# A product and its raw copy moved within a batch: the linear branch of a fused attention kernel

## The chip, the cores and the metric

The kernel runs on one core of a Trainium2 chip. Its time is the device time of one execution in microseconds. Five engines of the core work side by side, each through its own list of instructions in order, and wait for each other with semaphores: TensorE (PE: matrix products, writes PSUM), VectorE (DVE), ScalarE (ACT), GpSimd (POOL) and SyncE (SP, which issues the DMAs).

## The reference

32 batches of x (256 rows of 128 channels). Each batch is normalised, goes through an attention with 16 heads of 8 channels, and through one of eight dense layers, and both are added to x. The attention has two branches over the same q, k and v. Cut to these:

```python
q = _layernorm(q, q_gamma, q_beta)
k = _layernorm(k, k_gamma, k_beta)
scores = jnp.einsum('bhnd,bhmd->bhnm', q, k) / jnp.sqrt(jnp.float32(D))
aw = jax.nn.softmax(scores, axis=-1)
kth = jax.lax.top_k(aw, topk)[0][..., -1:]          # topk = 12 of 256
aws = aw * (aw >= kth)
o_s = jnp.einsum('bhnm,bhmd->bhnd', aws / (aws.sum(-1, keepdims=True) + 1e-08), v)
qf = jax.nn.softmax(q, axis=-1)
kf = jax.nn.softmax(k, axis=-1)
kv = jnp.einsum('bhnd,bhne->bhde', kf, v)
z = jnp.einsum('bhnd,bhd->bhn', qf, kf.sum(axis=2))
o_l = jnp.einsum('bhnd,bhde->bhne', qf, kv) / (z[..., None] + 1e-06)
o = a * o_s + (1.0 - a) * o_l
return o @ Wproj.T + bproj
```

The sparse branch (o_s) keeps the 12 largest of 256 weights in each row. The linear branch (o_l) has no scores: its numerator and its z are one product of the query features qf with kv, the "linear product" below.

## The kernel before, in words

The kernel is written out engine by engine. For each engine a function `body(it, par, xr)` is called for it = -2 to 31, and in it a loop runs over eight slots, u_ = 0 to 7. The order of the work is the order of the statements in these functions; nothing else schedules it. In one slot, four tiles of scores (two heads, two halves of the rows, 128x256 each) pass each stage.

What the engines do in a slot, for the work that matters here:

- VectorE: MAX8 over the four score tiles (`top`, line 656), then for the tiles of the slot before: replace the eight largest (`rest`, 663, with a load of the eight values `e8`) and MAX8 over what is left (`next8`, 669). Slot 2 also masks kv (line 677), slot 3 also takes a maximum of qkn (682).
- GpSimd: `drop` = top minus its own first element (414), then `gap` and `below` (439, 443), a flag for each weight that is not kept. In slots 0 to 3 it also normalises q and k of the next batch (355, 361), the last step of which writes `qkn` in slot 3.
- ScalarE: a copy `kept` of the turned tiles (841), slot by slot different copies out of PSUM, four exponentials `e` with their row sums (881), the exponentials `e8` of the eight largest (886), then more copies, and its share of `below` (956).
- TensorE: `turn(u_)` transposes the weights of four slots ago and puts the dropped ones far below zero (1051, 1052), in every second slot `product(u_)` multiplies the kept weights with v (1073), then `early(u_)`, the scores for the next slot (1033), and `late(u_)`.

One PSUM bank, `work_ps`, serves in turn for a row of small products that the batch needs beside its scores: qf turned (slot 0), kv (slot 1), the linear product (line 1176), the transposes of qkn for the next batch (1186, slot 3), remainders of a split into bf16 parts, v, the next x turned, and the next q and k (1155, slot 7). Each writer waits for the one before it to have been copied out. For the linear product the semaphores are: `kv_ready` (VectorE has masked kv), `w_lin` (TensorE is done), `lin_copied` (ScalarE has copied the bank into `lin_raw`, a part of the tensor `over`, line 859). The transposes of qkn wait for `lin_copied` and for `qkn_ready` of GpSimd. ScalarE copies them into `part` (865), and SyncE's DMAs write the parts to memory and load them back as the queries and keys of the next batch.

Of the kernel before, what the change touches and what calls it, by code (L numbers as in the profile page):

```python
# [30 lines left out]
P = 128  # L31
H = 16
# [3 lines left out]
NT = N // P  # L36
# [11 lines left out]
VA = D + 1  # L48
# [22 lines left out]
def wait(engine, semaphore, value):  # L71

    if isinstance(value, int) and value <= 0:
        return None
    return engine.wait_ge(semaphore, value)
# [9 lines left out]
def build(nc, x, Wqkv, bqkv, q_gamma, q_beta, k_gamma, k_beta, alpha, Wproj, bproj, W, bW, logits, u, y):  # L85
# [12 lines left out]
    def exists(batch):  # L98
        return not isinstance(batch, int) or 0 <= batch < B

    with ExitStack() as ctx:
# [68 lines left out]
        kv = sb("kv", [P, H, VA])  # L170
        qfT = sb("qfT", [P, N])
# [3 lines left out]
        sums_sb, lin_raw = over[:, 0:NT * H], over[:, NT * H:2 * NT * H]  # L175
# [11 lines left out]
        e = sb("e", [P, RING, TILES, N])  # L187
# [14 lines left out]
        work_ps = ps("work_ps", [P, 512])  # L202
# [578 lines left out]
        def _(act):  # L781
# [48 lines left out]
            def body(it, par, xr):  # L830
                nxt = 1 - par
                for u_ in range(UNITS):
# [20 lines left out]
                        nc.scalar.copy(osT[:], pv_ps[:, 0:N]).then_inc(s["osT_copied"], 1)  # L853
                    if u_ == 1 and (exists(it + 1) or exists(it + 2)):
                        rsqrt_steps(it)
                    if u_ == 3 and exists(it):
                        act.wait_ge(s["w_lin"], it + 1)
                        wait(act, s["lin_ready"], it)
                        nc.scalar.copy(lin_raw.rearrange("p g e -> p (g e)"), work_ps[:, 0:NT * H * VA]).then_inc(
                            s["lin_copied"], 1)  # L860
                    if u_ == 4 and exists(it + 1):

                        act.wait_ge(s["w_qkT"], it + 2)
# [9 lines left out]
                    if exists(it):  # L873
# [11 lines left out]

                        nc.scalar.activation(e8[:, u_ % 2], drop[:, u_ % 2, :, 1:9], ACT.Exp).then_inc(s["e8_ready"], 1)  # L886

                    if u_ in (0, 4) and exists(it - 1):
                        act.wait_ge(s["pv_ready"], it * QUADS + (u_ - 6) // 2 + 1)

                        if u_ == 0:
                            wait(act, s["w_turn"], it - 2)
                        nc.scalar.copy(oT[:, nxt, u_ // 4].rearrange("p a n -> p (a n)"), pv_ps[:]).then_inc(
                            s["pv_copied"], 1)
# [112 lines left out]
        def _(pe):  # L1007
# [8 lines left out]
            def body(it, par, xr):  # L1016
# [61 lines left out]
                def sums():  # L1078

                    pe.wait_ge(s["pv_copied"], QUADS // 2 * it)  # L1080
                    for t in range(NT):
                        for q in range(QUADS):
                            at = (t * QUADS + q) * 4 * VA
                            mm(pv_ps[:, at:at + P], oT[:, nxt, q // 2, 1 - q % 2, t * P:(t + 1) * P], gather[:],
                               start=(t == 0 and q == 0), stop=False, is_transpose=True, skip_group_check=True)
                    if it == 1:
                        pe.wait_ge(s["eps_ready"], 1)
                    mm(pv_ps[:, 0:NT * H * VA].rearrange("p (g e) -> p g e", e=VA)[:, :, D], eps_ident[:],
                       z[:, nxt].rearrange("p t h -> p (t h)"), start=False, stop=True,
                       skip_group_check=True).then_inc(s["w_turn"], 1)  # L1090


                def remainder(p):
# [2 lines left out]
                    mm(work_ps[:], minus_one[:], part[:, p].rearrange("p a n -> p (a n)"), start=False,  # L1096
                       stop=True, skip_group_check=True).then_inc(s["w_rest"], 1)

                def early(u_):
                    if u_ == 0 and exists(it):  # L1100

                        pe.wait_ge(s["dexp_ready"], it + 1)
                        if exists(it + 1):
                            pe.wait_ge(s["raw_ready"], it + 2)
                        else:
                            pe.wait_ge(s["v_copied"], it + 1)
                        for t in range(NT):
                            last = nc.tensor.transpose(work_ps[:, t * P:(t + 1) * P], qk_exp[:, par, t, 0, :], ident[:])
                        last.then_inc(s["w_qfT"], 1)
                    if u_ == 1 and exists(it - 2):  # L1110

                        pe.wait_ge(s["osp_ready"], it - 1)
                        pe.wait_ge(s["lin_ready"], it - 1)
                        pe.wait_ge(s["pv_copied"], QUADS // 2 * it - 1 if exists(it - 1) else QUADS // 2 * B)
                        for t in range(NT):
                            dst = pv_ps[:, t * P:(t + 1) * P]
                            mm(dst, o_sparse[:, t, :], ident[:], start=True, stop=False, is_transpose=True)
                            last = mm(dst, lin[:, par, t, :], ident[:], start=False, stop=True, is_transpose=True)
                        last.then_inc(s["w_osT"], 1)
                    if u_ == 3 and exists(it - 2):  # L1120

                        pe.wait_ge(s["osT_copied"], it - 1)
                        pe.wait_ge(s["bout_ready"], 1)
                        pe.wait_ge(res_loaded[par], 16 * ((it - 2) // 2 + 1))
                        for t in range(NT):
                            dst = pv_ps[:, t * C:(t + 1) * C]
                            mm(dst, ident[:], x_res[:, par, t, :], start=True, stop=False)
                            mm(dst, xnT[:, (xr - 2) % XRING, t * P:(t + 1) * P], w_sel[:], start=False, stop=False)
                            mm(dst, ones3[:], bias3[:, 3 * C:4 * C], start=False, stop=False)
                            last = mm(dst, osT[:, t * P:(t + 1) * P], w_proj[:], start=False, stop=True)  # L1130
                        last.then_inc(s["w_out"], 1)
                    if u_ == 5 and exists(it + 1):

                        remainder(1)
                    if u_ == 6 and exists(it + 1):

                        if it == -1:
                            pe.wait_ge(s["wv_ready"], 1)
                            pe.wait_ge(s["bv_ready"], 1)
                        pe.wait_ge(s["part_ready"], PARTS * (it + 2))  # L1140
                        for t in range(NT):
                            dst = work_ps[:, t * C:(t + 1) * C]
                            mm(dst, xnT[:, (xr + 1) % XRING, t * P:(t + 1) * P], w_v[:], start=True, stop=False)  # L1143
                            last = mm(dst, ones3[:], bias3[:, 2 * C:3 * C], start=False, stop=True)
                        last.then_inc(s["w_v_ready"], 1)
                    if u_ == 7 and exists(it + 2):

                        pe.wait_ge(s["xT_copied"], it + 4)
                        if it == -2:
                            pe.wait_ge(s["wqk_ready"], 1)  # L1150
                            pe.wait_ge(s["pool_const"], 7)
                            pe.wait_ge(s["gather_ready"], 4)
                        for t in range(NT):
                            dst = work_ps[:, t * 2 * C:(t + 1) * 2 * C]
                            mm(dst, xnT[:, (xr + 2) % XRING, t * P:(t + 1) * P], w_qk[:], start=True, stop=False)  # L1155
                            if it == -2 and t == 0:
                                pe.wait_ge(s["bqk_ready"], 1)
                            last = mm(dst, ones3[:], bias3[:, 0:2 * C], start=False, stop=True)
                        last.then_inc(s["w_qk_ready"], 1)

                def late(u_):
                    if u_ == 1 and exists(it):
# [6 lines left out]
                        last = mm(work_ps[:, 0:H * VA], ones_row[:], eps_row[:].rearrange("o h e -> o (h e)"),  # L1169
                                  start=False, stop=True)  # L1170
                        last.then_inc(s["w_kv"], 1)
                    if u_ == 2 and exists(it):

                        pe.wait_ge(s["kv_ready"], it + 1)
                        for t in range(NT):
                            last = mm(work_ps[:, t * H * VA:(t + 1) * H * VA], qfT[:, t * P:(t + 1) * P],  # L1176
                                      kv[:].rearrange("p h e -> p (h e)"), start=True, stop=True)
                        last.then_inc(s["w_lin"], 1)
                    if u_ == 3 and exists(it + 1):

                        wait(pe, s["lin_copied"], it + 1)
# [39 lines left out]
                for u_ in range(UNITS):  # L1221
                    if exists(it if u_ >= 4 else it - 1):
                        turn(u_)
                    if u_ % 2 == 0 and exists(it if u_ >= 6 else it - 1):
                        product(u_)
                    if u_ == 5 and exists(it - 1):
                        sums()
                    early(u_)
                    if exists(it if u_ < UNITS - 1 else it + 1):
                        scores(u_)  # L1230
                    late(u_)
                    if (it, u_) == (-2, 7):
                        other_weights()
# [126 lines left out]
```

## Time and profile before

| | before |
|---|---|
| time, median of three runs | 1180.96 us (1179.04 to 1184.93) |
| time of the profiled execution | 1181.1 us |
| its span, first to last instruction | 1179.3 us |
| VectorE busy | 1148.9 us (97%) |
| ScalarE busy | 1063.5 us (90%) |
| GpSimd busy | 995.5 us (84%) |
| TensorE busy | 942.5 us (80%) |
| linear product on TensorE, idle before it | 40.4 us in 32 batches, released by VectorE's kv |
| transposes of qkn on TensorE, idle before them | 34.6 us, mostly released by GpSimd's qkn |
| copy of the linear product on ScalarE | 13.2 us in 32 batches, 411 ns each |
| mean granted TensorE clock | 0.992 of full speed |

All times below are from one profiled execution, in microseconds from the start of its span. "Busy" is the time in which an engine's instructions run; they overlap a little from one to the next, so starts are the safer numbers. The word behind an arrow in square brackets is what ended the idle time ahead of an instruction, as the profile infers it. A batch takes some 35 us of the span, a slot some 4.4.

### The profile page before, as it was taken

How to read it: one execution, taken by the hardware profiler on the slowest of the kernel's cores; microseconds unless marked ns; L12 is line 12 of the kernel's file. 1: busy time of each engine (PE TensorE's matmuls, PEld its weight loads, DVE VectorE, ACT ScalarE, POOL GpSimd, SP SyncE). 2: the span in 40 equal slices, each digit the busy share in tenths (PEclk: the TensorE clock that was granted, in tenths of full speed). 3: DMA queues.
4: the chain of work that ended last, by engine and by line, in shares of the span. 5: the costliest groups of instructions: out<-in, count | busy, mean ns of one | idle time of the engine just before them, and what ended most of it. 6: DMA issues, size and time to landing. Idle time of an engine off the chain costs nothing.

```text
span 1179.3 us, 34136 instructions
## 1 busy us (share of the span) xinstructions
PE 942.5 (80%) x9061; PEld 653.6 (55%) x9092; DVE 1148.9 (97%) x4358; ACT 1063.5 (90%) x3474; POOL 995.5 (84%) x1973
## 2 busy tenths in 40 slices
PE   4578878888888888888888888888887888888887
PEld 1355556555555555555555555555555555555555
DVE  7999999999999999999999999999999999999997
ACT  3689989999999999999999999999999989999986
POOL 6688888888889888889888888888888888889865
PEclk9999999999999999999999999999999999999999
DMA  3112321223321222231223231223221223321220
GB/s 100 46 55 82 86 86 38 77 61 86 87 84 39 70 68 86 86 87 37 77 60 86 86 86 45 70 59 86 86 86 48 67 61 86 86 82 38 71 63 13
DMA packets 165122, 82.74 MB, mean 70 GB/s; under 512 B 7737, under 2 KB 164927, under 8 KB 164930
## 3 DMA queue, kind: packets, MB, share of 16 engines
q1 hardware_dynamic: 164658, 80.43, 23.8%
q8 instruction: 74, 1.21, 0.4%
q14 instruction: 118, 0.97, 0.3%
q10 hardware_dynamic: 272, 0.13, 0.0%
HBM read 42.78 MB, written 37.75 MB: 68 GB/s over the span
## 4 chain that ended last, share of the span: by engine, by line
POOL 30%; ACT 24%; issue 18%; PE 17%; DVE 10%; DVEq 1%; POOLq 0%; DMA 0%; ACTq 0%; SPq 0%
ACT e L881 14%; POOL gap L439 10%; POOL below L443 5%; DVE top L656 4%; PE work_ps L1155 3%; DVE rest L663 3%; POOL qkn L361 3%; PE turn_ps L1051 3%; PE pv_ps L1073 3%; POOL qk_b L361 3%; POOL drop L414 2%; PE work_ps L1143 2%; POOL sq_half L424 2%; ACT part L910 2%; PE work_ps L1186 2%
## 5 line engine op out<-in xcount | busy, mean ns | idle before, releaser
L881 ACT ACTIVATE e<-score_ps,drop 128x256 f32<-128x256 f32 x1024 | 474.6, 492 | 32.3 <-POOL drop L414 32.2
L1051 PE MATMUL turn_ps<-ident,e 128*128 128x128 f32 x2016 | 382.9, 284 | 40.1 <-ACT kept L841 20.5
L663 DVE MATCH_REPLACE8 rest<-e 128x256 f32<-128x256 f32 x1020 | 411.6, 407 | 0.0
L669 DVE MAX8 next<-rest 128x8 f32<-128x256 f32 x1020 | 405.7, 413 | 0.5 <-issue 0.3
L656 DVE MAX8 top<-score_ps 128x8 f32<-128x256 f32 x1024 | 360.0, 413 | 10.2 <-PE score_ps L1033 10.0
L439 POOL TENSOR_SCALAR gap<-e,next 128x256 bf16<-128x256 f32 x794 | 368.9, 479 | 0.1
L1052 PE MATMUL turn_ps<-minus_huge,below 128*128 128x128 bf16 x2016 | 363.1, 221 | 0.0
L1051 PEld LDWEIGHTS turn_ps<-ident,e 128*128 128x128 f32 x2016 | 286.6, 142 | 72.4 <-issue 44.1
L841 ACT ACTIVATE kept<-turn_ps 128x1024 f32<-128x1024 f32 x252 | 266.9, 1059 | 36.6 <-PE turn_ps L1052 36.6
L443 POOL TENSOR_SCALAR below<-gap 128x768 bf16<-128x768 bf16 (+1 forms) x254 | 216.7, 853 | 41.7 <-POOL gap L439 41.7
L881 ACT ACTIVATION_READ_ACCUMULATOR e<-score_ps,drop 128x1 f32 x1024 | 230.6, 225 | 0.0
L1052 PEld LDWEIGHTS turn_ps<-minus_huge,below 128*128 128x128 bf16 x2016 | 215.1, 107 | 0.7
L1073 PE MATMUL pv_ps<-kept,v_aug 128*32 128x256 f32 x2000 | 134.9, 387 | 20.4 <-ACT over L900 20.2
L414 POOL TENSOR_TENSOR drop<-top 128x36 f32<-128x36 f32 x256 | 62.8, 245 | 91.9 <-DVE top L656 88.5
L956 ACT ACTIVATE below<-e,next 128x256 bf16<-128x256 f32 x222 | 123.7, 557 | 0.0
L1033 PE MATMUL score_ps<-k_slots,q_slots 64*128 64x256 bf16 x1024 | 103.0, 278 | 16.3 <-issue 10.1
L1073 PEld LDWEIGHTS pv_ps<-kept,v_aug 128*32 128x32 f32 x2000 | 55.0, 110 | 62.4 <-issue 42.8
L663 DVE MATCH_VALUE_LOAD rest<-e 128x8 f32 x1020 | 74.9, 73 | 3.4 <-ACT e L886 3.1
L1033 PEld LDWEIGHTS score_ps<-k_slots,q_slots 64*128 64x128 bf16 x1024 | 30.8, 94 | 72.4 <-issue 65.0
L886 ACT ACTIVATE e<-drop 128x32 f32<-128x32 f32 x256 | 66.6, 260 | 0.0
L1155 PE MATMUL work_ps<-w_qk,xnT 128*128 128x256 f32 x128 | 46.8, 449 | 20.4 <-ACT xnT L942 20.4
L1176 PE MATMUL work_ps<-kv,qfT 128*128 128x144 f32 x128 | 24.8, 317 | 40.4 <-DVE kv L677 40.4
(229 smaller groups left out, 1398.3 us busy)
## 6 DMA issues: line engine op xcount, KB each, us to landing
part_slots<-part SPq DMA_DIRECT2D x128, 192.0 KB, 2.3
q_slots<-part_slots SPq DMA_DIRECT2D x64, 256.0 KB, 3.4
k_slots<-part_slots SPq DMA_DIRECT2D x64, 256.0 KB, 3.9
part_slots<-part SPq DMA_DIRECT2D x64, 128.0 KB, 1.9
x_sb<-in_L_attn_x SPq DMA_DIRECT2D x32, 128.0 KB, 3.9
x_res<-in_L_attn_x SPq DMA_DIRECT2D x32, 128.0 KB, 4.0
out_y<-out_sb SPq DMA_DIRECT2D x32, 128.0 KB, 4.1
w_ops<-in_L_ffn_W SPq DMA_DIRECT2D x1, 512.0 KB
```

The lines of the kernel that those rows point to most:

```text
L439: nc.gpsimd.tensor_scalar(gap[:, half, t, :], e[:, r, t, :], -1.0, next8[:, r, t, TOPK - 9:TOPK - 8], ALU.mult, ALU.add).then_inc(s["gap_s ...
L443: nc.gpsimd.tensor_scalar(below[:, r, 0:many], gap[:, half, 0:many], HUGE, 0.0, ALU.min, ALU.max).then_inc(s["below_pool"], many)
L656: nc.vector.max(top[:, q, t, 1:9], score_ps[:, q, t // 2, t % 2, :]).then_inc(s["top_ready"], 1)
L663: nc.vector.match_replace(rest[:, t, :], e8[:, (u_ - 1) % 2, t, :], e[:, (u_ - 1) % RING, t, :], REMOVED).then_inc(s["rest_ready"], 1)
L669: nc.vector.max(next8[:, (u_ - 1) % RING, t, :], rest[:, t, :]).then_inc(s["next_ready"], 1)
L841: nc.scalar.activation(kept[:, u_ % 4], turn_ps[:], ACT.Relu).then_inc(s["turn_copied"], 1)
L881: nc.scalar.activation(e[:, u_ % RING, t, :], score_ps[:, u_ % 2, t // 2, t % 2, :], ACT.Exp, bias=drop[:, u_ % 2, t, 0:1], accum_out=z[:, ...
L956: nc.scalar.activation(below[:, r, t, :], e[:, r, t, :], ACT.Relu, scale=-1.0, bias=next8[:, r, t, TOPK - 9:TOPK - 8]).then_inc(s["below_a ...
L1033: last = mm(score_ps[:, v_ % 2, hh, nt, :], q_slots[rows, side, v_, nt * P:(nt + 1) * P], k_slots[rows, side, v_, :], start=True, stop=True)
L1051: mm(dst, e[:, r, t, keys], ident[:], start=True, stop=False, is_transpose=True)
L1052: last = mm(dst, below[:, r, t, keys], minus_huge[:], start=False, stop=True)
L1073: last = mm(pv_ps[32 * j:32 * (j + 1), half * N:(half + 1) * N], v_aug[:, side, mc, 4 * q + j, :], kept[:, v_ % 4, j % 2, mc, :], start=(m ...
```

## The change

The linear product leaves the end of TensorE's slot 2, where it stood in `late`, and becomes a function `linear` that is called in slot 3 behind `turn(3)` and ahead of `early(3)`, the output product of the batch two before. Its copy on ScalarE stays in slot 3 but moves from ahead of the four exponentials of that slot to behind them and behind `e8`.

```diff
@@ ScalarE, body
-                    if u_ == 3 and exists(it):
-                        act.wait_ge(s["w_lin"], it + 1)
-                        wait(act, s["lin_ready"], it)
-                        nc.scalar.copy(lin_raw.rearrange("p g e -> p (g e)"), work_ps[:, 0:NT * H * VA]).then_inc(
-                            s["lin_copied"], 1)
                     if u_ == 4 and exists(it + 1):
...
                         nc.scalar.activation(e8[:, u_ % 2], drop[:, u_ % 2, :, 1:9], ACT.Exp).then_inc(s["e8_ready"], 1)
 
+                    if u_ == 3 and exists(it):
+                        act.wait_ge(s["w_lin"], it + 1)
+                        wait(act, s["lin_ready"], it)
+                        nc.scalar.copy(lin_raw.rearrange("p g e -> p (g e)"), work_ps[:, 0:NT * H * VA]).then_inc(
+                            s["lin_copied"], 1)
@@ TensorE, body
+                def linear():
+
+                    pe.wait_ge(s["kv_ready"], it + 1)
+                    for t in range(NT):
+                        last = mm(work_ps[:, t * H * VA:(t + 1) * H * VA], qfT[:, t * P:(t + 1) * P],
+                                  kv[:].rearrange("p h e -> p (h e)"), start=True, stop=True)
+                    last.then_inc(s["w_lin"], 1)
...
-                    if u_ == 2 and exists(it):
-
-                        pe.wait_ge(s["kv_ready"], it + 1)
-                        for t in range(NT):
-                            last = mm(work_ps[:, t * H * VA:(t + 1) * H * VA], qfT[:, t * P:(t + 1) * P],
-                                      kv[:].rearrange("p h e -> p (h e)"), start=True, stop=True)
-                        last.then_inc(s["w_lin"], 1)
...
                     if u_ == 5 and exists(it - 1):
                         sums()
+                    if u_ == 3 and exists(it):
+                        linear()
                     early(u_)
```

On TensorE, from the scores that end slot 2 to the turn of slot 4, before (the names are output<-inputs; `kv,qfT` is the linear product, `x_res,ident` begins the output product, `ident,qkn` are the transposes of qkn; in square brackets the semaphores waited for):

```order
L1176 MATMUL work_ps<-kv,qfT 128x144 [waits kv_ready]
L1051 MATMUL turn_ps<-ident,e 128x128 [waits turn_copied,below_act,below_pool]
...
L1127 MATMUL pv_ps<-x_res,ident 128x128 [waits even_res_loaded,bout_ready,osT_copied]
...
L1033 MATMUL score_ps<-k_slots,q_slots 128x256 [waits exp_done,slots_loaded]
L1186 MATMUL work_ps<-ident,qkn 128x128 [waits qkn_ready,lin_copied]
L1051 MATMUL turn_ps<-ident,e 128x128 [waits turn_copied,below_act,below_pool]
```

The same stretch after:

```order
L1051 MATMUL turn_ps<-ident,e 128x128 [waits turn_copied,below_act,below_pool]
...
L1103 MATMUL work_ps<-kv,qfT 128x144 [waits kv_ready]
L1135 MATMUL pv_ps<-x_res,ident 128x128 [waits even_res_loaded,bout_ready,osT_copied]
...
L1033 MATMUL score_ps<-k_slots,q_slots 128x256 [waits exp_done,slots_loaded]
L1187 MATMUL work_ps<-ident,qkn 128x128 [waits qkn_ready,lin_copied]
L1051 MATMUL turn_ps<-ident,e 128x128 [waits turn_copied,below_act,below_pool]
```

The linear product has changed places with the turn of slot 3; the rest stands as before.

On ScalarE, slot 3 and the start of slot 4, before (`over<-work_ps` is the copy of the linear product):

```order
L841 ACTIVATE kept<-turn_ps 128x1024 [waits turn_ready,pv_ready]
L859 COPY over<-work_ps 128x288 [waits lin_ready,w_lin]
L881 ACTIVATE e,z<-score_ps,drop 128x256 [waits turn_ready,drop_ready]
...
L886 ACTIVATE e<-drop 128x32
L920 COPY out_sb<-pv_ps 128x256 [waits w_out]
```

After:

```order
L841 ACTIVATE kept<-turn_ps 128x1024 [waits turn_ready,pv_ready]
L876 ACTIVATE e,z<-score_ps,drop 128x256 [waits turn_ready,drop_ready]
...
L881 ACTIVATE e<-drop 128x32
L886 COPY over<-work_ps 128x288 [waits lin_ready,w_lin]
L920 COPY out_sb<-pv_ps 128x256 [waits w_out]
```

The copy has moved behind five instructions; before and after it, ScalarE's order is unchanged.

## Rows read from the trace of the kernel before

**Rows 1.** Busy time by stretch: length, PE, PEld, DVE, ACT, POOL, clock, DMA, GB/s

```profile
110.00:1125.00 1015.00, 830.15 (x8114) 579.32 (x8143) 1005.91 (x3836) 946.66 (x3092) 885.16 (x1747) 0.99 0.25 71
```

**Rows 2.** Waits of VectorE over the span: us in total, times, longest

```profile
DVE top L656 <- PE score_ps L1033: 10.0, 14, 2.7
DVE rest L663 <- ACT e L886: 3.1, 9, 0.6
```

**Rows 3.** Chain of waits, 614 to 634 us: start, us, what

```profile
614.56 1.23 POOL qkn L361
...
631.36 0.40 ACT xnT L942
631.80 0.70 PE work_ps L1155 x2
...
633.55 0.35 PE score_ps L1033 x4
```

**Rows 4.** Timeline of TensorE, slots 2 to 4 of one batch

```profile
610.63 0.76 PE L1176 MATMUL work_ps<-kv,qfT 128*128 128x144 f32 x4 [1.45 <-DVE kv L677]
611.22 0.27 PE L1051 MATMUL turn_ps<-ident,e 128*128 128x128 f32 x1
...
614.78 0.40 PE L1033 MATMUL score_ps<-k_slots,q_slots 64*128 64x256 bf16 x4
615.93 0.63 PE L1186 MATMUL work_ps<-ident,qkn 128*128 128x128 f32 x4 [0.76 <-POOL qkn L361]
...
617.86 1.07 PE L1073 MATMUL pv_ps<-kept,v_aug 128*32 128x256 f32 x16
```

**Rows 5.** Timeline of ScalarE in the same batch

```profile
608.92 1.03 ACT L841 ACTIVATE kept<-turn_ps 128x1024 f32<-128x1024 f32 x1
...
614.00 0.41 ACT L859 COPY over<-work_ps 128x288 f32<-128x288 f32 x1
614.59 0.47 ACT L881 ACTIVATE e<-score_ps,drop 128x256 f32<-128x256 f32 x1 [0.18 <-POOL drop L414]
...
616.52 0.38 ACT L920 COPY out_sb<-pv_ps 128x256 f32<-128x256 f32 x1
...
621.23 0.24 ACT L886 ACTIVATE e<-drop 128x32 f32<-128x32 f32 x1
...
630.98 0.25 ACT L886 ACTIVATE e<-drop 128x32 f32<-128x32 f32 x1
```

**Rows 6.** Timeline of VectorE: the batch's first row, two loads, the next batch

```profile
599.22 1.10 DVE L656 MAX8 top<-score_ps 128x8 f32<-128x256 f32 x3 [0.26 <-PE score_ps L1033]
...
622.92 0.07 DVE L663 MATCH_VALUE_LOAD rest<-e 128x8 f32 x1
...
631.40 0.09 DVE L663 MATCH_VALUE_LOAD rest<-e 128x8 f32 x1
...
634.30 1.08 DVE L656 MAX8 top<-score_ps 128x8 f32<-128x256 f32 x3
```

**Rows 7.** Timeline of TensorE: batch 1, and a wait near the end

```profile
77.69 0.76 PE L1176 MATMUL work_ps<-kv,qfT 128*128 128x144 f32 x4 [1.59 <-DVE kv L677]
...
82.99 1.08 PE L1186 MATMUL work_ps<-ident,qkn 128*128 128x128 f32 x4 [2.68 <-POOL qkn L361]
...
86.23 1.07 PE L1073 MATMUL pv_ps<-kept,v_aug 128*32 128x256 f32 x16
...
1129.64 0.40 PE L1033 MATMUL score_ps<-k_slots,q_slots 64*128 64x256 bf16 x4 [3.22 <-ACT e L881]
```

**Rows 8.** Busy time by stretch as in rows 1; the clock stands ahead of DMA

```profile
80.00:85.00 5.00, 2.32 (x15) 1.86 (x15) 5.00 (x19) 3.93 (x13) 4.68 (x8) 0.74 0.02 5
1130.00:1132.50 2.50, 2.50 (x18) 1.82 (x16) 2.37 (x10) 0.61 (x4) 1.32 (x4) 0.55 0.52 153
```

**Rows 9.** Timeline of VectorE: first rows of batch 1 and batch 2

```profile
66.31 1.08 DVE L656 MAX8 top<-score_ps 128x8 f32<-128x256 f32 x3
...
102.67 1.41 DVE L656 MAX8 top<-score_ps 128x8 f32<-128x256 f32 x4
```

## Prediction

> **What bounds the kernel now.** I read the busy time of the long middle first. From 110 to 1125 us VectorE is busy for 1005.91 of 1015 us [rows 1]: the selection (four MAX8, four replacements, four MAX8 in each of eight slots of a batch) runs nearly without a break. So whatever is gained elsewhere can bring at most the 9.1 us that are left there. The reader might stop at "VectorE is the bound" and conclude that TensorE and ScalarE have room. The second view speaks against that. VectorE's few waits are all on the other engines: 10.0 us on scores, 3.1 us on the exponentials of the eight largest [rows 2].
>
> How near is the other side? The chain of waits answers it for one batch [rows 3]: GpSimd's last step of the normalisation (qkn, ends 614.56 + 1.23 = 615.79), TensorE's transposes of qkn 0.14 us later at 615.93 [rows 4], then ScalarE's copies and exponentials and TensorE's products of slots 4 to 7 in turn, down to ScalarE's xnT copy (631.36 to 631.76), the query and key product that it releases at 631.80 and the next batch's first scores at 633.55. In the last slot of that batch VectorE loads the eight values at 631.40, and the ScalarE instruction that makes them runs from 630.98 to 631.23 [rows 5, 6]: 0.17 us before, about what a handover takes (0.14 us at the transposes, 0.04 us from the xnT copy to its product). So from qkn to the end of the batch there is **a second loop of about the same length as VectorE's own**. The batch from 599.22 to 634.30 [rows 6] lasts 35.08 us, with both near their limit. A delay inside that second loop is paid by VectorE.
>
> **Part 1: the product moves behind the turn of slot 3 (TensorE).** Before, the linear product waits 1.45 us for kv at 610.63 and the turn follows at 611.22 [rows 4]. The wait has VectorE's kv step as releaser, a step that the change doesn't touch. After, the turn goes first. Its last input is the kept copy of slot 2, ScalarE 608.92 to 609.95 [rows 5]; with 0.14 us for the handover it starts at 610.09. kv is there before the turn is through, so the product (0.59 us, 610.63 to 611.22) follows at once; the turn and the output product take 611.22 to 614.78 = 3.56 us together, as now. The three end at 610.09 + 3.56 + 0.59 = 614.24, and the scores behind them (0.40 us) at 614.64. No instruction is added, no DMA moves, and TensorE has gained 0.54 us there. The gain comes to nothing, since what TensorE does next waits for something later (below), and the kept copy of slot 3, which the earlier turn releases, is followed on ScalarE by exponentials that wait for GpSimd anyway.
>
> **Part 2: the raw copy moves behind the exponentials of slot 3 (ScalarE).** Now it runs at 614.00 for 0.41 us, and the first exponential follows at 614.59 after 0.18 us of waiting for GpSimd's subtraction [rows 5]. That start is GpSimd's, so taking the copy away from the front does not bring the exponentials forward: the gain is 0. After, the copy takes the place that the output copy has now, right behind the eight values: 616.52 [rows 5], to 616.93. The output copy and one `below` slide by some 0.3 us into time in which ScalarE would wait for the turn of slot 4.
>
> **What waits for it.** The transposes of qkn write the PSUM bank that the copy reads, so TensorE waits there for `lin_copied` and for qkn. Before, the copy was over at 614.41 and qkn came last, at 615.79. After, the copy is last: 616.93 plus a handover of 0.04 to 0.14 us gives 616.97 to 617.07, against 615.93. I take 617.03, **1.10 us later in each batch** (bounds 1.04 and 1.14). Behind this wait stand, in TensorE's order, the turn of slot 4, the product and the scores of that slot; ScalarE's part copy, the exponentials of slot 4 and all that follows hang on the turn and the transposes. What is spare on the way is at the slot ends of VectorE, and in the last slot nothing is spare (above), so I count all of it. The change concerns the 31 batches that have a next one: 31 x 1.10 = 34.1 us.
>
> **What the longer wait does to TensorE's clock.** TensorE now waits 0.76 us before the transposes [rows 4]; after, from 614.64 to 617.03, 2.39 us, every batch. The trace has two waits above 2 us with the clock at its full level (2.4 GHz) before them: 2.68 us before 82.99 and 3.22 us before 1129.64 [rows 7]. In both places the granted clock then stands at the lower level of 1.2 GHz for some microseconds: 0.74 on the mean over 80 to 85 and 0.55 over 1130 to 1132.5 [rows 8]. The wait of 1.59 us before 77.69 was not followed by it: the linear product behind it has its usual 0.76 us [rows 4, 7]. 2.39 is nearer to 2.68, so I expect the fall in most batches.
>
> The price is in the same rows, since the wait at 82.99 is at this very place, in batch 1: from the start of the transposes to the product behind the turn it took 82.99 to 86.23 = 3.24 us, against 615.93 to 617.86 = 1.93 us at the full clock [rows 4, 7]: 1.31 us more. That batch is also a trial of the claim that a delay there is paid in full: from its first MAX8 to the next batch's it lasted 66.31 to 102.67 = 36.36 us [rows 9], 1.28 us above the 35.08 of the batch above. Where the clock falls only after the transposes have begun, part of the 1.31 is saved; at no fall all of it. I take three quarters, 1.0 us per batch: 31 x 1.0 = 31 us; bounds 0 and 31 x 1.31 = 40.6 us.
>
> The Trainium skill (TensorE: Matmul & The Clock Gate, section "What's actually happening") says that the ramp penalty is below 1% of a typical kernel's span, which would be under 11.8 us here. Batch 1 shows 1.31 us for one fall, and nothing in this trace shows many of them; by the page's rule the sum would be rival 1.
>
> **The sum.** The profiled execution took 1181.1 us (span 1179.3), beside a median of 1180.96. 1181.1 + 34.1 + 31 = 1246 us.
>
> **The rivals.**
> 1. *Late, but the clock holds or rarely falls.* For it: a wait of 1.59 us did not lower it, and 2.39 lies between; ahead of the wait stands the output product. Then 1181.1 + 34.1 = 1215, and with a fall in each fourth batch 1225 us. The page above is on this side.
> 2. *Faster.* The 1.45 us wait for kv and the copy ahead of the exponentials could have been what holds the batch, the copy then costing nothing behind. It decides itself at 615.79: if the exponentials of slot 3 and the copy are over by the time qkn is, the transposes are not late. They would have to end 1.1 us sooner, and their start is GpSimd's. At best VectorE's 9.1 us: 1172 us.
> 3. *VectorE has spare time enough.* The eight values of slot 4 are ready at 621.23 + 0.24 = 621.47 and are loaded at 622.92 [rows 5, 6], 1.45 us later, more than 1.10. If a later slot takes up the rest, the time stays within 1176 to 1187 us. Against it: the 0.17 us in the last slot, and batch 1. A half-way case (half of the delay taken up, no fall of the clock) gives 1198 us.
>
> **How the numbers follow.** The forecast, late with the clock falling in most batches (1226 to 1260): 0.62. Rival 1 (1208 to 1226): 0.23. The half-way case (1187 to 1208): 0.05. No change: 0.05. Faster: 0.03. Above 1260: 0.02. The range from 1210 to 1260 us holds some 0.84 of this: its low end is 31 x 1.04 = 32.2 us with a little taken up by VectorE's spare time, its high end 31 x (1.14 + 1.31) = 76 us, 1257, and a few us for other places. Faster or slower means by over 0.5%, about what a measurement of this kernel can tell from no change (1175 and 1187 us): faster 0.03, same 0.05, slower 0.92.
>
> **What the profile after would show.** TensorE's wait for kv is gone from the table of waits, and the turn of slot 3 starts right behind the kept copy of slot 2. The wait before the transposes of qkn is about 2.4 us and its releaser is ScalarE's copy, no longer GpSimd; the copy starts about 0.1 us behind the start of the eight values. VectorE's work stays as it is and its share of the span falls; its new waits are on ScalarE's eight values in the last three or four slots of a batch, about 2 us a batch. The row of the granted clock has values below 9, and its mean goes from 0.99 to about 0.95 (batch 1 lost 0.26 x 5 us in the stretch shown). Wrong would be: a copy that ends before qkn (step "what waits for it"), a wait of 2.4 us at an unchanged clock mean (the clock term), or batches still of 35.1 us though the transposes come 1.1 us late (the claim that all of it is paid).

## The result, and the profile after

The changed kernel takes 1244.91 us (median of four runs, 1241.1 to 1245.98) against 1181.8 us before: the ratio is 1.0522, with an interval of 1.05 to 1.0543. The change costs 63 us, some 2 us in each of the 31 batches that have a next one. The forecast was 1246.

The first view of the changed kernel is busy time by stretch, over the long middle and then over 8 us of one batch (that which begins at 479.35). The columns are those of [rows 1]; the clock is the third number from the end.

```profile
110.00:1185.00 1075.00, 868.10 (x8125) 601.33 (x8154) 1019.20 (x3846) 950.89 (x3097) 888.23 (x1751) 0.96 0.23 67
494.00:496.00 2.00, 1.03 (x9) 0.51 (x7) 2.00 (x11) 1.55 (x7) 2.00 (x4) 1.00 0.00 0
496.00:498.00 2.00, 0.90 (x7) 0.85 (x8) 2.00 (x6) 1.73 (x8) 1.84 (x4) 0.92 0.00 0
498.00:500.00 2.00, 2.00 (x15) 1.55 (x12) 2.00 (x10) 0.00 (x0) 1.80 (x5) 0.50 0.00 0
500.00:502.00 2.00, 2.00 (x22) 0.72 (x22) 1.79 (x8) 1.64 (x3) 1.83 (x5) 0.73 0.00 0
```

VectorE, nearly without a gap before (9.1 us of 1015, [rows 1]), now stands idle for 56 of 1075 us. The mean clock of the middle fell from 0.99 to 0.96, and the four short rows show how: TensorE works for half of 494 to 498, and from just before 498 to past 500 it is granted 0.50, the lower of its two levels.

The timeline of TensorE for the same batch answers to [rows 4]. In square brackets stand the idle time ahead and what ended it.

```profile
490.56 0.30 PE L1051 MATMUL turn_ps<-ident,e 128*128 128x128 f32 x1 [0.93 <-ACT kept L841]
...
491.96 0.71 PE L1103 MATMUL work_ps<-kv,qfT 128*128 128x144 f32 x4
...
494.64 0.40 PE L1033 MATMUL score_ps<-k_slots,q_slots 64*128 64x256 bf16 x4
497.10 0.66 PE L1187 MATMUL work_ps<-ident,qkn 128*128 128x128 f32 x4 [2.06 <-ACT over L886]
...
500.20 1.48 PE L1073 MATMUL pv_ps<-kept,v_aug 128*32 128x256 f32 x16
```

The linear product no longer waits. The transposes do, 2.06 us instead of 0.76, and what ends their wait is ScalarE's copy, no longer GpSimd's qkn. The turn behind them runs at the lower level: the product follows 3.10 us after the transposes' start, not 1.93.

ScalarE in the same stretch, to hold beside [rows 5]:

```profile
489.38 1.03 ACT L841 ACTIVATE kept<-turn_ps 128x1024 f32<-128x1024 f32 x1
...
494.69 0.48 ACT L876 ACTIVATE e<-score_ps,drop 128x256 f32<-128x256 f32 x1 [0.45 <-POOL drop L414]
...
496.51 0.25 ACT L881 ACTIVATE e<-drop 128x32 f32<-128x32 f32 x1
496.63 0.42 ACT L886 COPY over<-work_ps 128x288 f32<-128x288 f32 x1
...
500.36 1.02 ACT L841 ACTIVATE kept<-turn_ps 128x1024 f32<-128x1024 f32 x1 [2.64 <-PE turn_ps L1052]
```

The exponentials still start when GpSimd lets them: ScalarE waits 0.45 us for it, where it copied before. The copy ends at 497.05, the transposes start 0.05 us later, and ScalarE then stands idle for 2.64 us until the turn of slot 4 is there.

VectorE's waits through the rest of this batch:

```profile
502.20 1.43 DVE L656 MAX8 top<-score_ps 128x8 f32<-128x256 f32 x4 [0.41 <-PE score_ps L1033]
503.99 0.09 DVE L663 MATCH_VALUE_LOAD rest<-e 128x8 f32 x1 [0.37 <-ACT e L881]
508.75 0.09 DVE L663 MATCH_VALUE_LOAD rest<-e 128x8 f32 x1 [0.45 <-ACT e L881]
513.77 0.09 DVE L663 MATCH_VALUE_LOAD rest<-e 128x8 f32 x1 [0.60 <-ACT e L881]
516.98 1.42 DVE L656 MAX8 top<-score_ps 128x8 f32<-128x256 f32 x4 [0.23 <-PE score_ps L1033]
```

They add up to 2.06 us in one batch, spread over its second half: each time VectorE has caught up with the loop that starts at the transposes. Over the whole span the table of waits says the same, beside [rows 2]:

```profile
PE work_ps L1187 <- ACT over L886: 66.9, 31, 4.1
...
DVE rest L663 <- ACT e L881: 44.5, 86, 1.2
...
DVE top L656 <- PE score_ps L1033: 16.6, 34, 2.7
```

VectorE's two waits grew from 13.1 to 61.1 us. Two things could be behind that 63 us, late transposes and a slower TensorE, and the profile of one kernel shows them together. The experiments take them apart.

### The profile page after: what moved, and what is told of

The parts are those of the page before. It is cut to its first block, busy times and chain, and to the rows that moved or that the text cites. A ratio compares the mean times of both kernels' runs of the same rounds, so it can differ in the third digit from the quotient of the medians.

```text
span 1239.4 us, 34136 instructions
## 1 busy us (share of the span) xinstructions
PE 979.8 (79%) x9061; PEld 675.0 (54%) x9092; DVE 1160.0 (94%) x4358; ACT 1066.0 (86%) x3474; POOL 995.6 (80%) x1973
## 4 chain that ended last, share of the span: by engine, by line
ACT 31%; POOL 22%; PE 20%; issue 17%; DVE 8%; DMA 1%; DVEq 1%; POOLq 0%; ACTq 0%; SPq 0%
ACT e L876 19%; POOL gap L439 8%; PE turn_ps L1051 5%; POOL below L443 4%; DVE top L656 3%; PE work_ps L1163 3%; PE pv_ps L1073 3%; ACT kept L841 2%; DVE rest L663 2%; POOL qk_b L361 2%; PE turn_ps L1052 2%; PE work_ps L1187 2%; PE work_ps L1151 2%; POOL drop L414 2%; ACT below L956 2%
## 5 line engine op out<-in xcount | busy, mean ns | idle before, releaser
L1051 PE MATMUL turn_ps<-ident,e 128*128 128x128 f32 x2016 | 410.6, 297 | 64.4 <-ACT kept L841 47.2
L1052 PE MATMUL turn_ps<-minus_huge,below 128*128 128x128 bf16 x2016 | 387.9, 229 | 0.0
L1051 PEld LDWEIGHTS turn_ps<-ident,e 128*128 128x128 f32 x2016 | 302.3, 150 | 116.5 <-issue 61.2
L876 ACT ACTIVATION_READ_ACCUMULATOR e<-score_ps,drop 128x1 f32 x1024 | 241.2, 236 | 0.0
L1052 PEld LDWEIGHTS turn_ps<-minus_huge,below 128*128 128x128 bf16 x2016 | 224.6, 111 | 1.1 <-issue 0.2
L1073 PE MATMUL pv_ps<-kept,v_aug 128*32 128x256 f32 x2000 | 141.8, 403 | 21.6 <-ACT over L900 20.4
L956 ACT ACTIVATE below<-e,next 128x256 bf16<-128x256 f32 x222 | 127.4, 574 | 0.0
L1187 PE MATMUL work_ps<-ident,qkn 128*128 128x128 f32 x128 | 27.1, 348 | 72.8 <-ACT over L886 66.9
L881 ACT ACTIVATE e<-drop 128x32 f32<-128x32 f32 x256 | 69.8, 272 | 0.0
```

Of the source, the lines that this page charges most:

```text
L876: nc.scalar.activation(e[:, u_ % RING, t, :], score_ps[:, u_ % 2, t // 2, t % 2, :], ACT.Exp, bias=drop[:, u_ % 2, t, 0:1], accum_out=z[:, ...
L956: nc.scalar.activation(below[:, r, t, :], e[:, r, t, :], ACT.Relu, scale=-1.0, bias=next8[:, r, t, TOPK - 9:TOPK - 8]).then_inc(s["below_a ...
L1051: mm(dst, e[:, r, t, keys], ident[:], start=True, stop=False, is_transpose=True)
L1052: last = mm(dst, below[:, r, t, keys], minus_huge[:], start=False, stop=True)
L1073: last = mm(pv_ps[32 * j:32 * (j + 1), half * N:(half + 1) * N], v_aug[:, side, mc, 4 * q + j, :], kept[:, v_ % 4, j % 2, mc, :], start=(m ...
```

## The experiments

The theory: the copy behind the exponentials makes the transposes about 1.05 us late, which VectorE pays in full; and the wait that this leaves on TensorE lowers its clock in most batches, at some 1 us each. Rival A: all of the loss is the lateness, and the low clock costs nothing. Rival B: the product's new place on TensorE does the harm.

### The two moves apart

**e1_product_only** has the product in its new place and the copy in its old one:

```diff
+                    if u_ == 3 and exists(it):
+                        act.wait_ge(s["w_lin"], it + 1)
+                        wait(act, s["lin_ready"], it)
+                        nc.scalar.copy(lin_raw.rearrange("p g e -> p (g e)"), work_ps[:, 0:NT * H * VA]).then_inc(
+                            s["lin_copied"], 1)
                     if u_ == 4 and exists(it + 1):
...
                         nc.scalar.activation(e8[:, u_ % 2], drop[:, u_ % 2, :, 1:9], ACT.Exp).then_inc(s["e8_ready"], 1)
 
-                    if u_ == 3 and exists(it):
-                        act.wait_ge(s["w_lin"], it + 1)
-                        wait(act, s["lin_ready"], it)
-                        nc.scalar.copy(lin_raw.rearrange("p g e -> p (g e)"), work_ps[:, 0:NT * H * VA]).then_inc(
-                            s["lin_copied"], 1)
```

> Product in slot 3 behind the turn as in the changed kernel, its copy back ahead of the exponentials. Theory (late copy, then the clock): the product is over at 612.04 on the time axis of the prediction, ScalarE is free for the copy at 614.0 as before, the transposes of qkn wait for GpSimd again; 1181 us, +-5, clock mean 0.99. Rival (the product's new place holds TensorE up): 1215 us or more.

Measured: 1184.74 us, ratio to before 1.0004 (0.9992 to 1.0017). The move on TensorE costs nothing and brings nothing that this measurement can tell. Rival B is out. In its table of waits the transposes wait for GpSimd as before:

```profile
PE work_ps L1187 <- POOL qkn L361: 41.2, 31, 3.1
```

**e2_copy_only** is the other half: the product stays in `late(2)`, only the copy moves.

```diff
-                    if u_ == 3 and exists(it):
-                        act.wait_ge(s["w_lin"], it + 1)
-                        wait(act, s["lin_ready"], it)
-                        nc.scalar.copy(lin_raw.rearrange("p g e -> p (g e)"), work_ps[:, 0:NT * H * VA]).then_inc(
-                            s["lin_copied"], 1)
                     if u_ == 4 and exists(it + 1):
...
                         nc.scalar.activation(e8[:, u_ % 2], drop[:, u_ % 2, :, 1:9], ACT.Exp).then_inc(s["e8_ready"], 1)
 
+                    if u_ == 3 and exists(it):
+                        act.wait_ge(s["w_lin"], it + 1)
+                        wait(act, s["lin_ready"], it)
+                        nc.scalar.copy(lin_raw.rearrange("p g e -> p (g e)"), work_ps[:, 0:NT * H * VA]).then_inc(
+                            s["lin_copied"], 1)
```

> Product in slot 2 as before, its copy behind the exponentials as in the changed kernel. Theory: transposes 1.05 us late in each batch, 33 us in all; TensorE's wait ahead of them only 1.85 us, since the product still waits for kv in slot 2, so the clock falls in fewer batches: 1215 to 1240 us, clock mean 0.96 to 0.985. Rival (all of the loss is the lateness and what hangs on it, the clock costs nothing): as the changed kernel, 1245 us. Rival (the product's place): 1181 us.

Measured: 1246.42 us, ratio 1.0516 (1.0498 to 1.0535). The whole loss belongs to the copy. My expectation was a few us too low: I had counted on fewer falls of the clock with a wait of 1.8 us. One batch on TensorE:

```profile
495.28 0.40 PE L1033 MATMUL score_ps<-k_slots,q_slots 64*128 64x256 bf16 x4
497.49 1.11 PE L1186 MATMUL work_ps<-ident,qkn 128*128 128x128 f32 x4 [1.82 <-ACT over L886]
...
500.92 1.07 PE L1073 MATMUL pv_ps<-kept,v_aug 128*32 128x256 f32 x16
```

After 1.82 us of waiting the four transposes take 1.11 us, much as at 82.99 (1.08 us, [rows 7]), and the product comes 3.43 us after their start. By its time alone this run would fit rival A as well.

### Lateness without the slow clock

**e3_filled_wait** is the changed kernel, in which TensorE has something to do while it waits: it makes the scores of slot 3 five times over, the same values in the same place.

```diff
-                    for t in range(TILES):
+                    for t in list(range(TILES)) * (5 if u_ == 3 and it >= 0 else 1):
                         hh, nt = t // 2, t % 2
```

> The changed kernel, with the four score products of slot 3 issued five times over (the same values in the same place), so that TensorE works through most of its wait ahead of the transposes; no instruction that the others wait for is later than 616.3, VectorE needs these scores at 617.4. Theory: the transposes are still 1.05 us late, but the wait is some 0.8 us and the clock stays: 1215 us, +-6, clock mean 0.985 or more. Rival (the clock costs nothing): 1245 us. If the clock falls all the same: 1245 us with a mean near 0.96, and the test says nothing.

Measured: 1218.36 us, ratio 1.0275 (1.0251 to 1.03). One batch on TensorE:

```profile
489.24 1.27 PE L1033 MATMUL score_ps<-k_slots,q_slots 64*128 64x256 bf16 x20
491.74 0.66 PE L1187 MATMUL work_ps<-ident,qkn 128*128 128x128 f32 x4 [1.23 <-ACT over L886]
...
493.70 1.07 PE L1073 MATMUL pv_ps<-kept,v_aug 128*32 128x256 f32 x16
```

The busy time of its middle, with the clock ahead of the DMA share:

```profile
110.00:1160.00 1050.00, 859.45 (x8581) 603.91 (x8612) 1014.68 (x3844) 950.25 (x3101) 889.88 (x1751) 0.99 0.24 69
```

The transposes are as late as in the changed kernel, but the wait ahead of them is 1.23 us (0.8 had been expected), the clock keeps its mean of 0.99, and the product follows after 1.96 us. With more instructions on TensorE it loses 34.2 us on before, where the changed kernel loses 63.1. Rival A is out: it wanted 1245 us. So is any loss in proportion to lateness alone, since the lateness is the same and the loss is half.

### The slow clock without lateness

**e4_idle_no_delay** is the kernel before with a shorter output product, so that TensorE idles ahead of transposes that come no later than before. It leaves x, the dense layer and the bias out of the output of batches 0 to 29.

```diff
-                            mm(dst, ident[:], x_res[:, par, t, :], start=True, stop=False)
-                            mm(dst, xnT[:, (xr - 2) % XRING, t * P:(t + 1) * P], w_sel[:], start=False, stop=False)
-                            mm(dst, ones3[:], bias3[:, 3 * C:4 * C], start=False, stop=False)
-                            last = mm(dst, osT[:, t * P:(t + 1) * P], w_proj[:], start=False, stop=True)
+                            last = mm(dst, osT[:, t * P:(t + 1) * P], w_proj[:], start=True, stop=True)
```

> The kernel before, with the output product of slot 3 cut to its two products with w_proj: x itself, the dense layer and the bias are left out of the output of batches 0 to 29. Product and copy stand as before, so the transposes are not late, but TensorE is idle some 2.4 us ahead of them. Theory: the clock falls in most batches and costs about 1 us in each: 1205 to 1222 us, clock mean 0.95 to 0.97. Rival (the clock costs nothing): 1181 us.

Measured: 1200.05 us, ratio 1.0144 (1.009 to 1.0197): with less work some 16 us slower than before. The mechanism is there, 5 us short of the range that I gave. TensorE in a batch in which the clock fell and in one in which it didn't:

```profile
372.12 0.63 PE L1183 MATMUL work_ps<-ident,qkn 128*128 128x128 f32 x4 [2.37 <-POOL qkn L361]
...
375.12 1.56 PE L1073 MATMUL pv_ps<-kept,v_aug 128*32 128x256 f32 x16
...
408.44 0.63 PE L1183 MATMUL work_ps<-ident,qkn 128*128 128x128 f32 x4 [2.38 <-POOL qkn L361]
410.36 1.07 PE L1073 MATMUL pv_ps<-kept,v_aug 128*32 128x256 f32 x16
```

The busy time by stretch around the first of the two:

```profile
370.00:372.50 2.50, 0.38 (x4) 0.41 (x5) 2.50 (x12) 2.32 (x9) 2.50 (x5) 1.00 0.00 0
372.50:375.00 2.50, 2.50 (x19) 1.93 (x17) 2.50 (x9) 1.01 (x5) 2.34 (x4) 0.55 0.00 0
```

The same wait, the same releaser, and yet 3.00 us against 1.92 from the transposes to the product. So the length of the wait does not decide alone whether the clock falls; that the product comes about 1 us later where it falls shows directly. What this does to the batch is better read from many than from these two: the first lasts 36.30 us (from one first MAX8 to the next) and the second 35.17, but the same two batches last 35.91 and 35.18 in the kernel before, where the clock falls in neither. Over all batches of this run, those with a late product are 0.88 us longer than the others (table below).

### How much lateness, how much wait

Two more kernels put the copy between the exponentials of slot 3, the product where the change has it: behind the second (t == 1, below) and behind the third (t == 2).

```diff
                                                 ).then_inc(s["exp_done"], 1)
+                            if u_ == 3 and t == 1:
+                                act.wait_ge(s["w_lin"], it + 1)
+                                wait(act, s["lin_ready"], it)
+                                nc.scalar.copy(lin_raw.rearrange("p g e -> p (g e)"), work_ps[:, 0:NT * H * VA]).then_inc(
+                                    s["lin_copied"], 1)
...
```

> The changed kernel with the copy between the second and the third of the four exponentials of slot 3. Theory: the copy starts at 615.51, ends at 615.92, and the transposes start at 616.0, 0.1 us late; TensorE waits 1.4 us ahead of them, less than the 1.59 us that passed without a fall: 1184 to 1190 us, clock mean 0.985 or more. Rival (loss in proportion to lateness, 60 us for 1.05 us): 1187 to 1190 us. Rival (what costs is the copy being anywhere behind the first exponential): 1245 us.

Measured for **e5_after_two**: 1186.92 us, ratio 1.0027 (1.001 to 1.0043). The last rival, 1245 us, is out; the loss in proportion to lateness is not told from the theory here.

> The changed kernel with the copy between the third and the fourth exponential of slot 3. Theory: copy from 615.96 to 616.37, transposes at 616.45, 0.5 us late, 16 us in all; TensorE waits 1.8 us, as long as with the copy alone moved, where the clock fell in most batches: another 15 to 31 us, 1212 to 1232 us, clock mean 0.955 to 0.975. Rival (loss in proportion to lateness): 1214 us. Rival (lateness alone, no clock): 1200 us with a mean of 0.985 or more.

Measured for **e6_after_three**: 1218.87 us, ratio 1.0293 (1.025 to 1.0336). Lateness alone is out (1200 us; the clock mean of the profiled execution is 0.970 and not 0.985). The 1214 us of the loss in proportion lie inside the interval, 1212.7 to 1222.8, so it is e3 and not this run that speaks against it. In both the copy is what ends the wait of the transposes. From the table of waits of e5:

```profile
PE work_ps L1187 <- ACT over L883: 37.4, 31, 3.1
```

And from that of e6, 12 us more in the 31 batches:

```profile
PE work_ps L1187 <- ACT over L883: 49.0, 31, 3.6
```

All eight kernels side by side, from the timelines of their profiled executions, batches 1 to 30; the times stand beside 1184.15 us of before for e1 to e4 and 1183.09 for e5 and e6. The time is the median of all executions; the other columns come from the profiled one, which lies above the median in e5 (1190.4 us) and below it in e6 (1210.5) and after (1241.1). The start of the transposes, counted from the batch's first MAX8, and the wait are medians over the batches; "slow" are the batches in which the product comes over 2.2 us after the transposes' start (1.92 to 1.96 at the full clock); the last two columns are mean lengths of a batch, from one first MAX8 to the next.

| kernel | time, us | transposes start | wait ahead of them | slow batches | length, slow | length, others |
|---|---|---|---|---|---|---|
| before | 1181.8 | +16.69 | 0.75 | 1 of 30 | 36.36 | 35.43 |
| e1, product only | 1184.7 | +16.72 | 1.19 | 2 | 36.52 | 35.41 |
| e5, after two | 1186.9 | +16.72 | 1.08 | 4 | 36.86 | 35.55 |
| e4, idle, no delay | 1200.1 | +16.71 | 2.37 | 19 | 36.43 | 35.55 |
| e3, filled wait | 1218.4 | +17.77 | 1.23 | 1 | 37.56 | 36.59 |
| e6, after three | 1218.9 | +17.17 | 1.52 | 12 | 36.95 | 36.08 |
| after | 1244.9 | +17.75 | 2.06 | 21 | 37.69 | 36.84 |
| e2, copy only | 1246.4 | +17.77 | 1.83 | 21 | 38.01 | 36.75 |

Read down the last column: among the batches that are not slow, 0.48 us of lateness (e6) makes a batch 0.65 us longer, 1.08 us (e3) makes it 1.16 us longer. These batches can still hold a fall of the clock in another place. In e3, 20 of the 30 hold none at all and last 36.42 us on the mean, against 35.31 in the 24 such batches of before: 1.10 us for 1.08 us of lateness. That is the first term, paid in full. (e6 has only four such batches, too few to say.) Read the two last columns across: a slow batch is 0.85 to 1.3 us longer than the others of its kernel. That is the second. Slow batches become common between waits of 1.1 us (4 in e5, which loses 3.8 us) and 1.5 us (12 in e6, which loses 35.8).

## Why the prediction was right

**What bounds the kernel.** The second loop, from qkn through TensorE and ScalarE to the end of the batch, was as long as VectorE's. e3 shows it most plainly: a TensorE that runs at its full clock, 1.08 us late in one place, makes each batch longer by that and nothing of it is taken up. Batch 1, which the prediction took for a trial of this, was a weak one: its 36.36 us are little more than the 36.12 us of the batch that begins at 138.35 in the same trace, in which the clock does not fall. Rival 3 (spare time) fails by the same run; the 1.45 us that VectorE had in slot 4 [rows 5, 6] was no help to slots 6 and 7.

**Part 1 and part 2.** As told. The product's move alone is worth nothing (e1, 1.0004), and the exponentials did not start sooner without the copy ahead of them: they wait 0.45 us for GpSimd. Rival 2 (faster) fell where the prediction said it would be decided: the copy ends at 17.70 us into the batch, qkn's end was at 615.79 - 599.22 = 16.57.

**What waits for it.** The forecast was 1.10 us per batch and 34.1 us in all. The transposes start 1.06 us later, and e3 against before measures the term: 1218.36 - 1184.15 = 34.2 us.

**The clock.** The forecast was 31 us; the changed kernel less e3, each against its own runs of before, leaves 63.1 - 34.2 = 28.9 us. The pieces were a little off in both directions. The wait is 2.06 us and not 2.39, mostly because the kept copy of slot 2, which starts the turn, stands 0.33 us later in the batch than before (its end is 489.38 + 1.03 - 479.35 = 11.06 us into the batch, as against 10.73). The slow batches are 21 of 30, where "three quarters" of the price stood for more; and the product in them comes 3.19 us after the transposes on the mean, 1.24 us late. 21 x 1.24 = 26 us, which is all that the profiled execution has to explain: it took 1241.1 us, and 1241.1 - 1181.8 - 34.2 = 25.1. In the lengths of batches the same sum is spread otherwise: the 21 with a late product are 0.85 us longer than the other nine, and these nine, at 36.84 us, are 0.25 us longer than those of e3, since more of them hold falls in other places. One is at the start of batch 28, whose product then comes 1.95 us behind the transposes, at the full clock again:

```profile
1078.47:1080.97 2.50, 2.50 (x16) 1.81 (x14) 2.50 (x10) 1.01 (x3) 0.87 (x2) 0.50 0.47 134
```

Rival 1 (the clock rarely falls, 1215 to 1225 us) is what e3 is, and the kernel as changed is not. The rule that stood on its side, that the ramp costs less than 1% of a typical kernel's span (the Trainium skill, TensorE: Matmul & The Clock Gate, "What's actually happening"), is no guide to this kernel, in which the clock falls again and again: 28.9 us are 2.4% of 1181.8.

What the working had thinnest was the step from two waits (2.68 and 3.22 us) to "most batches". It came out right, but e2 and e6 show that the waits need not be that long: at 1.83 us as many batches were slow as at 2.06, at 1.52 us still 12 of 30. I had taken the 1.59 us before 77.69 [rows 7] for a wait that passes without harm, and for e2 and e5 built expectations on that; it was one draw of many. The trace of before held the answer: at the start of a batch the clock falls around a wait of 1.00 us, with one of 0.65 us shortly ahead of it.

```profile
277.99 0.70 PE L1155 MATMUL work_ps<-w_qk,xnT 128*128 128x256 f32 x2 [0.65 <-ACT xnT L942]
280.74 0.61 PE L1033 MATMUL score_ps<-k_slots,q_slots 64*128 64x256 bf16 x4 [1.00 <-issue]
280.50:283.00 2.50, 2.26 (x15) 1.56 (x16) 1.54 (x7) 1.84 (x6) 1.11 (x2) 0.50 0.89 253
```

The same happens at 173.89 after 1.24 us and at 952.75 after 1.58 us. And "three quarters" was a choice between bounds of 0 and 40.6 us: that the sum came within 2 us of the measured time is in part luck; the mechanism with its two terms is what the runs show. Why the same 2.37 us lowers the clock in 19 batches of e4 and leaves it in 11 was not tried and stays open.

## What to carry to other kernels

An engine that is 97% busy does not make the others free: follow the chain of waits around one whole period, and if a second loop has the same length, a new wait inside it can be paid in full, as here, whatever the share of busy time says. A copy that empties a shared bank on such a loop belongs ahead of work that can wait, since the next writer of the bank stands in line, with all that is queued behind it on its engine. And price a new wait on TensorE twice: once for its length, and once for the clock of the work that comes behind it.

## What was not expected of the hardware

Work for nothing paid: 16 more score products in each batch cut the changed kernel's loss from 63.1 to 34.2 us, and less work made the kernel before 16 us slower (e4), both by way of TensorE's clock. The lower level was granted around waits of 1.0 us (280.74 in the kernel before), in 12 of 30 batches at 1.5 us (e6), and at 2.4 us it was still not certain (19 of 30 in e4).
